# A Mamba-2 layer and a ternary gated FFN: x goes to token order by VectorE blocks and DRAM instead of TensorE transposes

## The reference

```
zxbcdt = u @ W_in.T                      # z 1024, x 1024, B 64, C 64, dt 8
x, B, C = silu(causal_conv4(xBC))        # 4 taps per channel
dt = softplus(dt + dt_bias);  A = -exp(A_log)
y  = SSD(x*dt, A, B, C) + x*D            # 8 heads of 128, state 64, chunked scan
y  = rmsnorm(y * silu(z)) * norm_w
x1 = layernorm(u + y @ W_out.T)
```

## Time and profile before

| | |
|---|---|
| median of 3 runs | 1474.45 us (1472.0 to 1476.62) |
| the profiled execution | 1473.74 us, span 1471.7 us |
| busy in the span | TensorE 1447.2 us (98%), VectorE 1016.4 (69%), ScalarE 861.0 (59%), GpSimd 432.1 (29%) |
| mean granted TensorE clock | 0.995 of full |

### The profile page before, as it was taken

One profiled execution on the slowest core, in us unless ns is written; L12 is line 12 of the kernel. 1 busy time (PEld: TensorE's weight loads), 2 busy tenths in 40 slices (PEclk: granted clock), 3 DMA queues, 4 the chain that ended last, 5 costly groups with the idle time before them and its releaser, 6 DMA issues.

```text
span 1471.7 us, 26863 instructions
## 1 busy us (share of the span) xinstructions
PE 1447.2 (98%) x10132; PEld 1303.3 (89%) x10132; DVE 1016.4 (69%) x2219; ACT 861.0 (59%) x1655; POOL 432.1 (29%) x544
## 2 busy tenths in 40 slices
PE   9999999999999999999998999999999999999997
PEld 8889898889898888998976889999999999999996
DVE  6776686667766776678668987766565666666555
ACT  7876667576765676767762234545455454545443
POOL 5334554445435453354362106500000000000001
PEclk9999999999999999999999999999999999999999
DMA  7113312332233232332247333445353545445341
GB/s 272 65 48 97 101 52 80 87 101 84 65 98 87 80 86 55 99 100 59 87 132 255 108 115 123 166 136 167 112 179 101 158 122 165 130 126 169 100 136 66
DMA packets 141760, 168.05 MB, mean 114 GB/s; under 512 B 76480, under 2 KB 85184, under 8 KB 141632
## 3 DMA queue, kind: packets, MB, share of 16 engines
q1 hardware_dynamic: 141632, 166.35, 36.8%
HBM read 132.62 MB, written 33.69 MB: 113 GB/s over the span
## 4 chain that ended last, share of the span: by engine, by line
PE 89%; DMA 4%; DVE 3%; ACT 2%; issue 1%; SPq 1%; POOL 0%; DVEq 0%; ACTq 0%
PE ps L403 25%; PE ps L265 23%; PE ps L473 16%; PE ps L359 11%; PE ps L313 3%; PE ps L393 3%; DMA x_scratch<-s_rr 2%; PE ps L321 2%; PE ps L330 2%; PE ps L300 1%; DVE s_xact L841 1%; SPq L1406 1%; PE ps L233 1%; PE ps L286 1%; DMA s_rr<-in_un 0%
## 5 line engine op out<-in xcount | busy, mean ns | idle before, releaser
L403 PE MATMUL ps<-s_xoh,s_S 128*128 128x256 f32 x896 | 220.3, 281 | 0.1
L403 PE MATMUL ps<-s_xol,s_S 128*128 128x256 f32 x896 | 220.3, 282 | 0.0
L473 PE MATMUL ps<-s_tern,s_hh 128*128 128x512 f32 x504 | 199.2, 395 | 0.0
L473 PE MATMUL ps<-s_tern,s_hl 128*128 128x512 f32 x504 | 199.2, 395 | 0.0
L265 PE MATMUL ps<-s_uhi,s_whi 128*128 128x256 f32 x1088 | 180.7, 288 | 2.7 <-ACT s_uhi L543 2.7
L403 PEld LDWEIGHTS ps<-s_xoh,s_S 128*128 128x128 f32 x896 | 169.5, 189 | 5.9 <-issue 0.9
L265 PE MATMUL ps<-s_uhi,s_wlo 128*128 128x256 f32 x1088 | 174.5, 283 | 0.0
L265 PE MATMUL ps<-s_ulo,s_whi 128*128 128x256 f32 x1088 | 174.1, 282 | 0.0
L403 PEld LDWEIGHTS ps<-s_xol,s_S 128*128 128x128 f32 x896 | 169.4, 189 | 4.8
L1284 POOL TENSOR_TENSOR s_lnb<-s_lnb,s_cst 128x1 f32<-128x1 f32 x32 | 18.2, 572 | 497.0 <-DVE s_lnb L1131 497.0
L403 PE MATMUL ps<-s_xol,s_tern 128*128 128x256 f32 x672 | 163.7, 281 | 0.0
(11 more groups left out here) (182 smaller groups left out, 2986.2 us busy)
## 6 DMA issues: line engine op xcount, KB each, us to landing
s_S<-wsum_scratch SPq DMA_DIRECT2D x48, 512.0 KB, 3.6
s_S<-wsum_scratch SPq DMA_DIRECT2D x96, 256.0 KB, 3.4
s_bcx<-ct_scratch SPq DMA_DIRECT2D x32, 512.0 KB, 3.8
s_wst<-in_wffn SPq DMA_DIRECT2D x48, 256.0 KB, 2.8
s_wraw<-in_wffn SPq DMA_DIRECT2D x16, 768.0 KB, 8.1
s_uraw<-in_uT SPq DMA_DIRECT2D x16, 512.0 KB, 6.4
s_rr<-in_un SPq DMA_DIRECT2D x32, 256.0 KB, 3.1
x_scratch<-s_rr SPq DMA_DIRECT2D x32, 256.0 KB, 2.2
```

Of the source, the lines that this page charges most:

```text
L403: o = e.matmul(bank[:, 256 * mi:256 * mi + 256], wt(mi, k), xo[g % 2][:, x, k, :], start=(first and mi == 0 and k == 0 and xo is xoh), sto ...
L473: o = e.matmul(DB[c][:], y[:, 128 * c:128 * c + 128], tern[:, j, 1024:1536], start=(j == 0 and lo == 0), stop=(j == 15 and lo == 1))
```

## The change

TensorE's 64 `TR` steps and ScalarE's 64 `f_xTe` steps go. In their place, for each chunk: `f_xtr(c, 0)` and `(c, 1)` on VectorE transpose x by blocks of 32 by 32 into `xs` (one buffer), `store_xb(c)` writes `xs` to DRAM in four DMAs of 128 KB, in runs of 1 KB, and `load_xT(c)` reads 512 KB back into `xT` (now 2 buffers). For this the x channels are permuted in the split weights: `raw_in` places each raw x tile as strips of 32 columns in four split tiles, so each x tile of the product needs four raw tiles (`parts_of`). The raw x tiles land in `xr`, which lies over `xw` and `mm`; `f_seg` and `f_xw` of the first chunks wait until all are split (`x_split`). The convolution's parameters come permuted too (`conv_par`, 16 small DMAs).

`DT` and `dtT` go from `MISC` to a bank of `Y` (`B0[1]`). `f_x1` goes from VectorE to ScalarE (a second small operation on GpSimd makes its bias). The block transposes of x1 for chunks 12 to 31 go from the mixer to the pairs: `load_xr` reads x1 back from DRAM into `xtt`, `f_xt2` transposes, `store_xt2` writes. The order of the steps on every engine is written anew; `warm` now stands behind `dtT(0)`, and `DT(0)` ahead of `ip(0, 0)`.

```diff
-    xT, o_xT = sb("xT", [128, 3, 8, 128])
+    xT, o_xT = sb("xT", [128, 2, 8, 128])
+    xs, _ = sb("xs", [128, 4, 8, 32])
     xw, o_xw = sb("xw", [128, 2, 8, 128])
+    xr, _ = sb("xr", [128, 8, 4, 128], F32, o_xw)
...
+    def parts_of(j):
+        return [8 + (j - 8) // 4 + 2 * q for q in range(4)] if 8 <= j < 16 else [j]
...
         def DT(m):
...
-            w.wait_ge(d_par, 48)
+            w.wait_ge(d_par, 64)
             if m:
-                w.wait_ge(s_ms, 4 * m - 2)
-                w.wait_ge(s_GM, 2 * m)
+                w.wait_ge(s_gate[1], 4 * m - 2)
...
-        def TR(c, half):
...
-                o = e.transpose(B0[half][:, 128 * i:128 * i + 128],
-                                xact[:, 4 * half + i, 128 * (c % 2):128 * (c % 2) + 128], ident)
...
         def Y(c):
             w.wait_ge(s_DI, c + 1)
+            xT_landed(w, c)
...
-        warm(); ip(0, 0); DT(0); dtT(0); ip(0, 1); ip(0, 2); ip(0, 3); CUM(0); ip(0, 4); ip(0, 5); G(0); ip(0, 6)
+        DT(0); ip(0, 0); ip(0, 1); dtT(0); warm(); ip(0, 2); CUM(0); ip(0, 3); ip(0, 4); ip(0, 5); ip(0, 6); G(0)
...
-            DT(m); OP(c - 1); ip(n, 0); ip(n, 1); dtT(m); ip(n, 2); Y(c); CUM(m); ip(n, 3); ST(c); G(n); ip(n, 4)
+            DT(m); dtT(m); ip(n, 0); ip(n, 1); OP(c - 1); ip(n, 2); Y(c); CUM(m); ip(n, 3); ST(c); G(n); ip(n, 4)
+            OP(c); Y(c + 1); SQ(c); ip(n, 5); ip(n, 6); ip(n, 7); ip(n, 8); ST(c + 1); SQ(c + 1); OP(c + 1)
+            ip(n + 1, 0); ip(n + 1, 1); ip(n + 1, 2); ip(n + 1, 3); Y(c + 2); ip(n + 1, 4); ip(n + 1, 5); G(n + 1)
+            ST(c + 2); OP(c + 2); Y(c + 3); SQ(c + 2); ST(c + 3); ip(n + 1, 6); ip(n + 1, 7); ip(n + 1, 8); SQ(c + 3)
...
-        def f_xTe(c, half):
...
+        def f_x1(c):                                          # ScalarE
+            v, r = lnb[:, c % 2, :], rr[:, c % 3, :]
+            w.wait_ge(s_rs1, 2 * c + 2)
+            e.activation(r, r, AF.Identity, scale=v[:, 11:12], bias=v[:, 12:13]).then_inc(s_x1, 1)
...
+        split_in(8); split_in(16); split_in(10); f_uhi(0); expA(); f_xe(0, 0); split_in(14); split_in(13)
+        split_in(12); split_in(9); split_in(15); split_in(0); split_in(11); f_spexp(0); f_silc(0, 0); f_xe(0, 1)
...
+        def f_xtr(c, a):                                      # VectorE
+            w.wait_ge(s_silc, 5 * (c // 2) + 2 * a + 3)
+            if c:
+                w.wait_ge(d_xb, 64 * c)
+            e.transpose(xs[:, :, 4 * a:4 * a + 4, :].rearrange("p i h b -> p h i b"),
+                        xact[:, 4 * a:4 * a + 4, 128 * (c % 2):128 * (c % 2) + 128].rearrange(
+                            "p h (i t) -> p h i t", i=4)).then_inc(s_xtr, 1)
...
+        split_in(8); f_ulo(0); setup(); split_in(16); split_in(12); split_in(10); split_in(14); f_taps(0, 0); f_dte(0)
...
+            f_ms(c - 1); f_dte(m); f_ulo(n); f_dtr(m)
...
+            f_gate(c + 1, 0); f_xtr(c + 2, 0); f_xtr(c + 2, 1); f_dd(c + 2); f_gate(c + 1, 1); f_xtr(c + 3, 0)
+            f_ms(c); f_xtr(c + 3, 1); f_sqsum(c + 1); f_r1(c); f_wz(c + 2); f_ms(c + 1); f_S(c + 1)
...
+            f_ms(c + 2); f_gate(c + 3, 0); f_gate(c + 3, 1); f_r1(c + 2); f_xtr(c + 4, 1)
+            if m < NG // 2 - 1:
+                f_dd(c + 5)
+            f_sqsum(c + 3)
+            if m <= 3:
+                f_xt(c + 1)
+            f_S(c + 3); f_xtr(c + 5, 0)
...
+            f_xtr(c + 5, 1)
...
+        def load_xr(c):                                       # SP
...
+            e.dma_start(xtt[:], x1d[128 * c:128 * c + 128, :]).then_inc(d_xs, 16)
...
+        def store_xb(c):
+            w.wait_ge(s_xtr, 2 * c + 2)
+            for j in range(4):
+                e.dma_start(xbd[c, :, :, j, :],
+                            xs[32 * j:32 * j + 32].rearrange("p i h b -> p i (h b)")).then_inc(d_xb, 16)
+
+        def load_xT(c):
+            w.wait_ge(d_xb, 64 * c + 64)
+            if c >= 2:
+                w.wait_ge(s_Y, c - 1)
+                w.wait_ge(s_xw, c - 1)
+            e.dma_start(xT[:, c % 2].rearrange("p h s -> p (h s)"),
+                        xbd[c].rearrange("a i j f -> i a (j f)")).then_inc(d_xT[c % 2], 16)
...
+            store_x1(c + 1); store_xb(c + 4); load_r0(c + 3); load_xT(c + 4); store_x1(c + 2); store_xb(c + 5)
             if m < NG // 2 - 1:
                 store_ct(m + 1)
...
+            load_xT(c + 5)
```

More of the change, by code:

```diff
@@ L210, in build_program, with last_of, raw_in, x_split @@
     XQ = ((X11, 0, 0), (D3, 0, 1), (X21, 1, 0), (X22, 1, 1))
+    def parts_of(j):
+        return [8 + (j - 8) // 4 + 2 * q for q in range(4)] if 8 <= j < 16 else [j]
+    def last_of(order, tiles):
+        return max([order.index(j) + 1 for j in tiles if j in order] + [0])
+    def raw_in(j):
+        if j < 8 or j == 16:
+            return wlr[:, j, :, :], whi[:, j, :, :], wlo[:, j, :, :]
+        q, a = (j - 8) // 2, j % 2
+        t = slice(8 + 4 * a, 12 + 4 * a)
+        return (xr[:, j - 8, :, :].rearrange("p k (i b) -> p i k b", i=4),
+                whi[:, t, :, 32 * q:32 * q + 32], wlo[:, t, :, 32 * q:32 * q + 32])
+    def x_split(w):
+        w.wait_ge(s_whi, last_of(WHI_ORDER, range(8, 16)))
+        w.wait_ge(s_wlo, last_of(DVE_LO, range(8, 16)))
+        w.wait_ge(s_wlop, last_of(POOL_LO, range(8, 16)))
+    def xT_landed(w, c):
+        w.wait_ge(d_xT[c % 2], 16 * (c // 2 + 1))
+    def x1_count(c):
+        return sum(80 if i < 12 else 16 for i in range(c % 3, c + 1, 3))
     def x1_stored(w, c):
-        w.wait_ge(d_x1[c % 3], 80 * (c // 3 + 1))
+        w.wait_ge(d_x1[c % 3], x1_count(c))
     def program_pe(e):
@@ L237, in dtT @@
         def dtT(m):
[L238 removed]
+            w.wait_ge(d_par, 64)
             w.wait_ge(s_dte, m + 1)
             for c in range(4):
[L241 removed]
+                i = e.transpose(B0[1][:, 128 * c:128 * c + 128], dts[:, 128 * c:128 * c + 128], ident)
             i.then_inc(s_dtT, 1)
@@ L290, in G @@
             i.then_inc(s_G, 1)
-        def TR(c, half):
[L293 to L299, removed]
-                o = e.transpose(B0[half][:, 128 * i:128 * i + 128],
-                                xact[:, 4 * half + i, 128 * (c % 2):128 * (c % 2) + 128], ident)
-            o.then_inc(s_TR[half], 1)
         def Y(c):
             w.wait_ge(s_DI, c + 1)
-            later = c + 1 if c % 2 else c + 2
+            xT_landed(w, c)
             for half in range(2):
-                w.wait_ge(s_xTe[half], later)
-                if c % 2:
-                    w.wait_ge(s_gate[half], c)
+                w.wait_ge(s_gate[half], c)
+            if c == 0 or c % 4 == 2 and c < NCH - 2:
+                w.wait_ge(s_neg, (c + 2) // 4 + 1)
             for a in range(2):
                 for i in range(4):
-                    o = e.matmul(B0[a][:, 128 * i:128 * i + 128], xT[:, c % 3, 4 * a + i, :], mm[:, c % 2, 4 * a + i, :],
+                    o = e.matmul(B0[a][:, 128 * i:128 * i + 128], xT[:, c % 2, 4 * a + i, :], mm[:, c % 2, 4 * a + i, :],
                                  start=(i == 0), stop=fresh(c) and i == 3, skip_group_check=True)
@@ L1182, in program_dve @@
                 f_h21(Q - 1); f_h12(Q - 1)
+            if Q % 2 == 1 and Q < 40:
+                f_xt2(12 + Q // 2)
             if p == 2:
@@ L1408, in store_xt, with store_xt2 @@
                             ).then_inc(d_x1[c % 3], 16)
+        def load_xr(c):
+            x1_stored(w, c)
+            w.wait_ge(s_dtT, NG // 2)
+            w.wait_ge(d_ct, 16 * (NG // 2))
+            w.wait_ge(d_xs, 80 * (c - 12))
+            e.dma_start(xtt[:], x1d[128 * c:128 * c + 128, :]).then_inc(d_xs, 16)
+        def store_xt2(c):
+            w.wait_ge(s_xt, c + 1)
+            for i in range(4):
+                e.dma_start(xtd[c // 2, :, :, 4 * (c % 2) + i, :],
+                            xtt[32 * i:32 * i + 32, :].rearrange("a (f b) -> a f b", b=32)).then_inc(d_xs, 16)
         def load_xt0():
@@ L1423, in load_xt @@
             X, kh, h = XQ[i]
-            for c in range(4 * g, 4 * g + 4):
-                x1_stored(w, c)
+            if g < 3:
+                for c in range(4 * g, 4 * g + 4):
+                    x1_stored(w, c)
+            else:
+                w.wait_ge(d_xs, 80 * (4 * g + 2 * h - 10))
             if g == 1:
@@ new lines, in program_sp @@
+            if m <= 3:
+                store_xt(c - 2)
+            load_wst(3 * n + 1); load_bc(c + 2); store_xb(c + 2); load_r0(c + 1); load_wst(3 * n + 2); load_xT(c + 2)
+            load_bc(c + 3); store_xb(c + 3); store_x1(c - 1); load_wst(3 * n + 3); load_bc(c + 4); load_wst(3 * n + 4)
+            if m <= 3:
+                store_xt(c - 1)
+            load_r0(c + 2)
+            if m == NG // 2 - 1:
+                load_xt0()
+            load_xT(c + 3); load_bc(c + 5); load_wst(3 * n + 5)
```

300 lines of the change are left out of this document (162 added, 138 removed).

## The result

The changed kernel takes **1507.3 us** (median of 4 runs, 1503.97 to 1509.8) against 1475.53 of the kernel before on the same chips (1472.0 to 1476.69, 4 runs): a ratio of **1.0218**, 95% interval 1.0187 to 1.0249. It is slower by 32 us where 1452 was forecast, and lies outside the range. The profiled execution took 1509.59 us, its span 1507.6.

The account below looks back on a forecast made before the run. TensorE was taken as the bound, 98% busy. Terms -31.0 + 6.1 - 4.4 + 3 + 7 - 3 = -22.3 from 1473.74 give 1451.4; the runs' median lies 0.7 higher, so 1452 us, range 1440 to 1467.

Parts of the forecast that it names:

- The transposes: TensorE's queue: 256 transposes of x leave it, eight taking 0.97 us from start to start; -31.0 us.
- The step that failed: DRAM round trip of x: xT's load takes 6.4 us at most, gate to landing 13.6, before Y needs it after over 20.
- the start: TensorE's first steps in their new order: ip(0, 3) begins at 26 to 33 us; net +7 us (3 to 11).
- The middle of the period: VectorE's wait for the xs store ahead of sqsum(c+1): 10.4 us against TensorE's 12.5, hidden with 2.1 to spare.
- The rival "Slower": Main loop: stores queue behind large loads on SP, land 4.2 us later, cost 42 us at dtT and SQ(c+1); 1494; chance 0.08.
- None of 128 such stores took over 3.8: Argument against stores landing as late as 6.4 us: the earlier profile's small 64 KB stores landed in 2.1 to 3.8 us.
- slow OP: Main loop: OP matmuls slowed behind the longest DT wait return to speed; 1.3 us of the -4.4.
- The +3 for odd waits: Main loop: a new order on five engines has its own odd waits, about as many as before; +3 us (0 to 8).
- f_xtr took 0.70 us for 0.71: VectorE's new block transposes of x, 64 of 128 x 512, were put at 0.71 us each, at most twice that.
- dtT waited seven times 0.87: Main loop: dtT directly behind DT waits 0.87 us for f_dte in each of seven periods; +6.1 us.
- DT's waits: Main loop: DT no longer waits for ms in MISC, so 3.1 us of TensorE's waits go, part of the -4.4.
- the pairs: After the mixer: 20 added block transposes cost VectorE 14 us, TensorE 0, up to +4 if loads of sum weights are held up.
- The mixer's end: Last Y and OP: waits of 1.40 us for xT's eviction and 1.64 behind r1 go; -3 us (0 to -4).

Follow-up runs that it names:

- load in order: The changed kernel with x's DRAM scratch laid out so that a chunk's load of xT is one 512 KB block in order; 1453.35 us, ratio 0.986.

## Why the prediction was wrong

Three stretches, cut where DT(1) and DT(7) begin (before 83.24 and 663.14, changed 96.80 and 696.11, load in order 89.03 and 647.65) and at the spans (1471.7, 1507.6, 1451.7), differ from the kernel before by:

| stretch | predicted | changed | load in order |
|---|---|---|---|
| to DT(1) | 7 - 3.9 = +3.1 | +13.6 | +5.8 |
| DT(1) to DT(7) | -23.3 + 5.2 - 4.4 + 3 = -19.5 | +19.4 | -21.3 |
| DT(7) to the end | -3.9 + 0.9 - 3 = -6.0 | +2.9 | -4.5 |
| sum | -22.4 | +35.9 | -20.0 |

(The transposes are shared out at 0.97 us a chunk: 4 chunks, 24 and 4.)

**The step that failed** is "Then load_xT, 512 KB: 6.4 us at the most by the uraw row [...] So xT itself comes in time." The load was priced by its bytes, by a load whose outermost dimension is not 4, and only as far as xT itself is concerned; what it does to the other DMAs on the queue was put at nothing, without a reason. Its transfer alone, 5.5 us, was within the 6.4. What the runs show in its place: it books a quarter of the DMA engines for 5.5 us, and r's store, bc and, in a few places, xT come late behind it. Alone it is worth 54 us, 1507.3 to 1453.35. Between DT(1) and DT(7) it is 40.7 us (19.4 + 21.3, table): 26.3 are idle time of TensorE (31.6 against 5.3), and 14.4 are matmuls that take longer (busy 567.75 against 553.37 us for the same 4090), at a granted clock of 0.98 against 1.00.

Without this load the forecast of 1452 would have held, with some luck: the start was 2.7 us dearer than forecast, the loop 1.8 cheaper, and the end gained 1.5 less.

**The middle of the period**, "hidden, with 2.1 us to spare", was reckoned for SQ(c+1) alone. f_xt, f_dd and f_ulo stand behind the same place of VectorE's list, and the waits that counted were f_xt's for r's store, up to 6.4 us, and f_dd's for bc, up to 5.1, not that for xs. The stores of xs landed in 3.0 us, median; the prediction allowed 2.2.

**The rival "Slower"** had the sign and more than half of the loss (1494), through stores late on the one queue; it was given 0.08. Its mechanism was half right: the stores of xs were not the late ones (3.0 us in the median), and the late ones were late not behind large loads as such but behind one that keeps few engines busy. "None of 128 such stores took over 3.8" was no evidence: those rows say nothing of what such a load does to the stores behind it.

**The start** was under-sized. With the transposes that leave it, the stretch to DT(1) cost +5.8 even with the load in order, forecast +3.1, so that the start itself cost 9.7 for 7, within its range of 3 to 11; in the changed kernel the stretch cost +13.6. TensorE's first rows there:

```profile
9.97 1.93 PE L272 MATMUL ps<-s_uraw,s_wdr 128*32 128x512 f32 x8 [9.97 <-DMA s_uraw<-in_uT]
...
16.98 0.73 PE L303 MATMUL ps<-s_uhi,s_whi 128*128 128x256 f32 x4 [2.21 <-ACT s_whi L556]
...
29.07 0.75 PE L303 MATMUL ps<-s_uhi,s_whi 128*128 128x256 f32 x4
...
63.40 2.90 PE L342 MATMUL ps<-s_mm,s_xT 128*128 128x128 f32 x12 [4.27 <-issue]
```

ip(0, 3) begins at 29.07, within 26 to 33 as reckoned. Y(0) then idles 4.27 us; the load of its xT was issued at 52.41. That and the rest up to +13.6 is again the load: with it in order the wait is gone.

**What held.** The transposes left TensorE at about their reckoned price: with the load in order TensorE is busy for 22.9 us less between DT(1) and DT(7) (576.30 before, 553.37), where 23.3 and 1.3 of slow OP were reckoned. The +3 for odd waits in the loop didn't come: the 5.3 us of idle time left there are the waits of dtT. f_xtr took 0.70 us for 0.71. dtT waited seven times 0.87. DT's waits went. With the load in order the pairs hide the 20 block transposes; after 880 us TensorE is busy for 562.82 of 571.7 us. The mixer's end gained 2.2 us of the 3 once xT came in time (from DT(7) to the last OP 130.3 us, 135.5 before, of which 3.9 - 0.9 are transposes and dtT): the last OP's wait of 1.64 went, but the OP ahead of it waited 2.28 where it had waited 1.54. In the changed kernel ST waited there up to 4.0 us for xw, which needs xT.

## What to carry to other kernels

Price a DMA by its shape as well as its bytes: look at the outermost dimension of both sides before trusting a row of the same size (here 32 and 128 spread over the engines, 4 and 2 did not). Then price what it does to those behind it on the queue: a transfer that comes in time itself can still make every later store late. And where an engine waits in order for a landing, check all that stands behind the wait, not only the next step that was thought of.

## What the runs showed of the hardware

- A load of 512 KB with 4 outermost blocks ran at a DMA share of 0.27 and 94 GB/s; two loads of 256 KB with 2 blocks each at 0.13 and 51 GB/s together; in order, at 0.90 and 351 GB/s. The cost in this kernel was 54 us and 170 us.
- Two DMAs with 2 blocks each, out at once, didn't use different engines: their share together was 0.13, two engines of 16. The Trainium skill's rule under "The theory" ("DMA: Bandwidth & Descriptors", section "Why a DMA increments its semaphore by 16 and not by 1") has both on the lowest-numbered engines; the share agrees that they were the same, and no profile here shows which.
- The profile gives no landing for the loads with 4 or 2 blocks, and one for those that spread (4.0 and 3.0 us).
